# A float32-accurate attention layer on one core: short products placed one by one, and the value products in halves

## The chip, the cores and the metric

The kernel runs on one core of a Trainium2 chip. A core has five engines with queues of their own: TensorE (matrix products into PSUM), VectorE, ScalarE, GpSimd and SyncE, which here issues nearly all DMAs. The metric is the device time of one execution in microseconds. Before the change it was 1571.13 us, the median of three runs (1570.92 to 1571.68).

## The reference

```
w = weights[conditions]                     # 32 of 200 matrices, 128 x 128
x = x + einsum('bct,bcd->bdt', x, w)        # x: 32 x 128 x 1024
# attention over the result: 16 heads of 64, sequence 128
q, k, v = (heads(einsum('bsd,ed->bse', x, W)) for W in (Wq, Wk, Wv))
scores = (q * min(precision, 4)) @ k^T / sqrt(64), causal mask
out = softmax(scores) @ v, heads side by side
x = x + einsum('bsd,ed->bse', out, Wo)      # result: 32 x 128 x 1024, float32
```

## The kernel before

Every float32 operand of a product is split into a high and a low part of the type that TensorE takes at full rate. A product then is three: high by high, high by low, low by high, added up in PSUM (`three`, lines 709 to 712). In most of them 128 rows of weights meet 512 moving columns; these write the banks `PJ` in turn.

TensorE's queue has four stretches. First, for each of the 32 batches, the product by the chosen matrix and its transposition by TensorE (`pe_l0_b`, line 841: a half batch is four transposes of 128 columns into one bank, 256 in all), mixed with the products for V of the first batches. Then the products for V of the other batches, in pairs of batches with seven sums in place of eight (`pe_v_step`), again with transposes in between. Then attention, in 64 cells: a cell is one quarter of the heads' channels of one group of four batches. It has eight steps for Q and eight for K, a step being one `three` of 512 columns, 0.68 us. Beside the steps stand the scores of the cell before (`pe_scores`: four blocks of three products of 256 columns into `SC`) and the value products of an earlier one (`pe_values`, line 815). Last, the output product for one group in full (`pe_out_step`) and for the others in pairs (`pe_product`), which end the kernel.

The value products: P, the normalised exponentials, is turned by VectorE and by DMAs, then split by ScalarE into its high part (L1045) and by GpSimd into its low part (L1336), which stand side by side in `PS`. For each block `u` and each half `h` of the heads one product has V's columns as weights and 256 moving columns, 128 of P's high and 128 of P's low part. PSUM then holds two results side by side, for V's high and low parts in different rows. ScalarE copies "the other rows" (`AC`, L1052 and L1053), VectorE adds the two 128-column results of "the own rows" (L1229, a reduction of 512 elements to 256), GpSimd adds `AC` (L1339), and SyncE stores the sum (L1656). `P` also numbers pairs of blocks: 128 pairs, 512 value products.

What stands where in a queue is set by a table of times: `At.put(t, item)` notes an item at time t in steps, and each engine's program walks over all ticks (`TICK` of them in a step) and issues what is due, in a fixed order of kinds. These times only set the order; on the chip each engine goes on as its semaphores allow. `T_END` is the step at which the steps of Q and K end, `a` the time from which a cell's scores and softmax are counted.

## Time and profile before

| | |
|---|---|
| median of three runs | 1571.13 us |
| span of the profiled execution | 1569.4 us |
| TensorE products, busy | 1559.1 us, 7563 instructions |
| TensorE weight loads, busy | 1311.9 us, 7563 instructions |
| VectorE, ScalarE, GpSimd, busy | 980.4, 818.9, 856.6 us |
| DMA | 341.46 MB, mean 218 GB/s |

The profile is of one execution. PE is TensorE's products, PEld its weight loads, which overlap the products; DVE is VectorE, ACT ScalarE, POOL GpSimd, SPq SyncE's queue of DMA issues. L815 is line 815 of the kernel. A product's duration runs from its start to its modelled end and overlaps the next one's.

### The profile page before, as it was taken

What the parts mean: (1) busy time and instruction counts of PE and PEld (TensorE: products, weight loads), DVE (VectorE), ACT (ScalarE), POOL (GpSimd) and SP (SyncE); (2) the same over time, 40 slices, a digit from 0 to 9 for tenths busy, and PEclk for the clock granted to TensorE, in tenths of its full rate; (3) what the DMA queues carried; (4) which work ended last, traced back from release to release, by engine and by line L of the source; (5) the groups of instructions that cost most, each with busy time, mean ns of one, the idle gap of its engine ahead of it and who ended that gap; (6) DMA issues with size and microseconds to landing.
All of it is one profiled execution on the core that took longest, in us unless ns stands there. A gap on an engine that the chain in (4) does not pass through costs nothing.

```text
span 1569.4 us, 23424 instructions
## 1 busy us (share of the span) xinstructions
PE 1559.1 (99%) x7563; PEld 1311.9 (84%) x7563; DVE 980.4 (62%) x1748; ACT 818.9 (52%) x2221; POOL 856.6 (55%) x752
## 2 busy tenths in 40 slices
PE   9999999999999999999999999999999999999999
PEld 7888888888888888888888888888888878888887
DVE  6844454443367777777766777777777754555553
ACT  6645545543366666666666666666666522222220
POOL 1545645643255566557555566675577544555552
PEclk9999999999999999999999999999999999999999
DMA  9958888865856766667677466666675696444442
GB/s 329 334 212 275 307 285 297 301 214 215 308 182 197 206 207 199 210 188 199 186 240 238 152 172 212 186 182 201 182 195 159 222 367 238 168 161 167 163 163 85
DMA packets 192299, 341.46 MB, mean 218 GB/s; under 512 B 23986, under 2 KB 116402, under 8 KB 185010
## 3 DMA queue, kind: packets, MB, share of 16 engines
q1 hardware_dynamic: 191026, 331.59, 65.8%
q10 hardware_dynamic: 1152, 8.39, 1.4%
q8 instruction: 60, 0.98, 0.3%
q14 instruction: 61, 0.50, 0.1%
HBM read 184.70 MB, written 134.22 MB: 203 GB/s over the span
## 4 chain that ended last, share of the span: by engine, by line
PE 98%; DMA 1%; SPq 1%; POOL 0%; issue 0%; DVE 0%; ACT 0%; DVEq 0%
PE p_PJ L710 22%; PE p_PJ L711 22%; PE p_PJ L712 22%; PE p_SC L712 6%; PE p_SC L711 6%; PE p_SC L710 6%; PE p_PV L815 4%; PE p_LP L710 1%; PE p_PV L710 1%; PE p_PV L712 1%; PE p_PV L711 1%; PE p_LP L711 1%; PE p_LP L712 1%; PE p_PV L841 1%; PE p_LP L841 1%; DMA out<-t_xr 1%
## 5 line engine op out<-in xcount | busy, mean ns | idle before, releaser
L711 PE MATMUL p_PJ<-t_XL,t_WH 128*128 128x512 f32 x1008 | 394.1, 391 | 0.0
L710 PE MATMUL p_PJ<-t_XH,t_WH 128*128 128x512 f32 x1008 | 394.1, 391 | 0.0
L712 PE MATMUL p_PJ<-t_XH,t_WL 128*128 128x512 f32 x1008 | 392.1, 389 | 0.0
L1035 ACT ACTIVATE t_PP<-t_PP,t_st 128x128 f32<-128x128 f32 x512 | 199.5, 391 | 175.4 <-DVE t_st L1211 173.9
L1333 POOL TENSOR_TENSOR t_PP<-t_PP,t_st 128x512 f32<-128x512 f32 x128 | 133.4, 1042 | 205.7 <-DVE t_st L1215 205.7
L712 PEld LDWEIGHTS p_PJ<-t_XH,t_WL 128*128 128x128 f32 x1008 | 189.3, 188 | 40.4
L710 PEld LDWEIGHTS p_PJ<-t_XH,t_WH 128*128 128x128 f32 x1008 | 190.0, 188 | 33.8
L711 PEld LDWEIGHTS p_PJ<-t_XL,t_WH 128*128 128x128 f32 x1008 | 190.0, 188 | 32.3
L1229 DVE TENSOR_REDUCE t_AT<-p_PV 64x256 f32<-64x512 f32 x252 | 171.2, 679 | 23.7 <-ACT t_AC L1053 12.0
L1339 POOL TENSOR_TENSOR t_AT<-t_AT,t_AC 128x256 f32<-128x256 f32 x126 | 117.2, 930 | 125.5 <-DVE t_AT L1229 125.5
L1336 POOL TENSOR_TENSOR t_PS<-t_PT,t_PS 128x512 fp32r<-128x512 f32 x122 | 157.7, 1293 | 0.0
L1205 DVE SCALAR_TENSOR_TENSOR t_PP<-p_SC,t_beta,t_mask 128x256 f32<-128x256 f32 x256 | 111.6, 478 | 44.4 <-PE p_SC L712 44.4
L1322 POOL TENSOR_TENSOR t_xl<-t_XT,t_xh 128x512 fp32r<-128x512 f32 x56 | 74.0, 1322 | 94.9 <-ACT t_xh L917 94.2
L1215 DVE RECIPROCAL t_st<-t_st 128x4 f32<-128x4 f32 x128 | 22.9, 179 | 142.0 <-ACT t_PP L1035 142.0
L1022 ACT ACTIVATE t_KH<-p_PJ 64x512 fp32r<-64x512 f32 x128 | 76.1, 595 | 47.8 <-PE p_PJ L712 46.2
L1052 ACT ACTIVATE t_AC<-p_PV 64x256 f32<-64x256 f32 x128 | 48.9, 382 | 95.9 <-PE p_PV L815 94.4
L1035 ACT ACTIVATION_READ_ACCUMULATOR t_PP<-t_PP,t_st 128x1 f32 x512 | 95.6, 187 | 0.0
L1327 POOL TENSOR_TENSOR t_VV<-t_VX,t_VV 128x512 fp32r<-128x512 f32 x64 | 81.4, 1293 | 25.2 <-ACT t_VV L999 25.2
L1192 DVE TENSOR_TENSOR t_KL<-p_PJ,t_KH 64x512 fp32r<-64x512 f32 x128 | 88.2, 689 | 11.0 <-ACT t_KH L1022 7.0
L1211 DVE TENSOR_REDUCE t_st<-t_PP 128x2 f32<-128x256 f32 x256 | 94.2, 409 | 0.0
L815 PE MATMUL p_PV<-t_PS,t_VV 128*128 128x256 f32 x512 | 82.8, 285 | 3.7 <-POOL t_PS L1336 3.7
L815 PEld LDWEIGHTS p_PV<-t_PS,t_VV 128*128 128x128 f32 x512 | 75.2, 192 | 9.3 <-POOL t_PS L1336 4.1
(254 smaller groups left out, 3545.8 us busy)
## 6 DMA issues: line engine op xcount, KB each, us to landing
t_XH<-xth_scratch SPq DMA_DIRECT2D x56, 512.0 KB, 6.5
t_XL<-xtl_scratch SPq DMA_DIRECT2D x56, 512.0 KB, 6.9
t_PT<-t_TB SPq DMA_DIRECT2D x580, 32.0 KB, 2.3
v_scratch<-t_VR SPq DMA_DIRECT2D x64, 256.0 KB, 4.5
xth_scratch<-t_XH SPq DMA_DIRECT2D x16, 1024.0 KB, 4.0
xtl_scratch<-t_XL SPq DMA_DIRECT2D x16, 1024.0 KB, 6.5
t_VX<-v_scratch SPq DMA_DIRECT2D x32, 512.0 KB, 5.7
at_scratch<-t_AT SPq DMA_DIRECT2D x126, 128.0 KB, 3.5
```

The costliest lines, as they stand in the source:

```text
L710: pe.matmul(bank, lh, rh, start=first, stop=False, skip_group_check=goes_on)
L711: pe.matmul(bank, lh, rl, start=False, stop=False, skip_group_check=goes_on)
L712: return pe.matmul(bank, ll, rh, start=False, stop=last, skip_group_check=goes_on)
L815: mm = pe.matmul(PV2[:, z, 256 * h:256 * h + 256], VV[j % 2][:, u, 2 * c + h, :], moving, start=True, stop=True)
L1035: act.activation(PP[:, u, h, :], PP[:, u, h, :], ACT.Exp, bias=st[:, 0, u, h:h + 1], scale=1.0, accum_out=st[:, 1, u, h:h + 1]).then_inc(a ...
L1192: dve.tensor_tensor(KL[r, :, k], pj[r], KH[r, :, k].bitcast(f32), ALU.subtract).then_inc(dve_k, 1)
L1205: dve.scalar_tensor_tensor(out=PP[:, u], in0=SC[u // 2][:, 256 * (u % 2):256 * (u % 2) + 256].rearrange("p (h k) -> p h k", h=2), scalar=b ...
L1211: dve.tensor_reduce(st[:, 0, u, :], PP[:, u], AX, ALU.max, negate=True).then_inc(dve_m, 1)
L1229: dve.tensor_reduce(at_tile(P)[r], both, AX, ALU.add).then_inc(dve_M, 1)
L1333: pool.tensor_tensor(pp, pp, r, ALU.mult).then_inc(pool_n, 1)
L1336: pool.tensor_tensor(p_half(P, 1), p_raw(P), p_half(P, 0).bitcast(f32), ALU.subtract).then_inc(pool_pt, 1)
L1339: pool.tensor_tensor(at_tile(P), at_tile(P), AC[:, P % 2], ALU.add).then_inc(pool_at, 1)
```

## The change

1. A step is cut into twelve ticks (before four), and each of its three products has a time of its own, a third of a step apart. The output steps get their times from the table too.
2. The transposes, the products of the score blocks and the value products are put into it one by one, a third of a step apart and (by `BETWEEN`) a sixth behind a 512-column product. A cell's scores now take four steps, one block each; the times counted from `a` are one step later. The first eight transposes stay in a row.
3. A value product of 256 columns becomes two of 128, over P's high and then P's low part, with the same weights, added up in the same 128 columns of PSUM. Each pair of blocks has one bank of 512 columns, in turn, where before both banks were shared by all; TensorE waits for the pair before the last, not for the last.
4. VectorE adds the own rows, now 256 columns, and ScalarE's copy of the other rows in one instruction. GpSimd's addition is gone, and with it the semaphore `at_out`; those that waited for it wait for `at_rows`.
5. VectorE's first turn of cell 58 waits for the loads of P as the other cells do, besides the weights' stores.

```diff
 NPAIR = (NG - 1) * GB // 2
 T_OUT = T_PAIR + NPAIR * PAIR
-TICK = 4
+TICK = 12
 T_START = -14
+
+BETWEEN = 1 / 6
...
                     block(kind, n)
                     for d in range(DC):
-                        step_at.put(t0 + 16 * c + 8 * i + d, (kind, n, d))
+                        for m in range(3):
+                            step_at.put(t0 + 16 * c + 8 * i + d + m / 3, (kind, n, d, m))
                 done = t0 + 16 * c + 8
...
                 kl_ev.put(done + 1, n)
-                a = done + 5
+                a = done + 6
                 for u in range(GB):
                     k = u // 2
-                    sc_at.put(a + k, GB * n + u)
+                    for m in range(3):
+                        sc_at.put(a - 1 + u + BETWEEN + m / 3, (GB * n + u, m))
                     mask_at.put(a + 1 + 2 * k, GB * n + u)
                     exp_at.put(a + (2, 3, 4, 5)[u], GB * n + u)
                 move_at.put(a + 10, n)
@@ -390,10 +399,10 @@
                     half_at.put(a + (20 if last else 25.25) + 0.5 * k, P)
                     ptl_at.put(a + (20.75 if last else 26) + 1.5 * k, P)
                     v = a + (27.25 + 3.25 * k if last else 29 + 4.5 * k)
-                    own = v + (1.75 if n >= 4 * NGRP - 2 else (1.75, 8.5)[k])
-                    for z in range(2):
-                        pv_at.put(v, 2 * P + z)
-                    other_at.put(v + 0.75, P)
+                    own = v + (3.25 if n >= 4 * NGRP - 2 else (3.25, 8.5)[k])
+                    for i in range(8):
+                        pv_at.put(v + BETWEEN + i / 3, (2 * P + i // 4, i // 2 % 2, i % 2))
+                    other_at.put(v + 2.25, P)
                     own_at.put(own, P)
                     at_at.put(own + 1.25, P)
 
...
             y_low.put(t + 12.75, b)
 
         turns = [(b, half) for half in (1, 0) for b in range(GB)]
-        x1_load = At()
+        x1_load, out_step, out_add = At(), At(), At()
         for o in range(N_OUT):
+            for d in range(DC):
+                for m in range(3):
+                    out_step.put(T_END + 8 * o + d + m / 3, (o, d, m))
+            out_add.put(T_END + 8 * o + 7.75, o)
...
 
 
+        def value_bank(P):
+
+            return PV[P % 2].rearrange("p (u h q) -> p u h q", u=2, h=2)
...
-        def three(bank, lh, ll, rh, rl, first, last, goes_on=False):
-            pe.matmul(bank, lh, rh, start=first, stop=False, skip_group_check=goes_on)
-            pe.matmul(bank, lh, rl, start=False, stop=False, skip_group_check=goes_on)
+        def one(m, bank, lh, ll, rh, rl, first, last, goes_on=False):
+
+            if m == 0:
+                return pe.matmul(bank, lh, rh, start=first, stop=False, skip_group_check=goes_on)
+            if m == 1:
+                return pe.matmul(bank, lh, rl, start=False, stop=False, skip_group_check=goes_on)
             return pe.matmul(bank, ll, rh, start=False, stop=last, skip_group_check=goes_on)
 
-        def pe_plain_v(n, d):
+        def three(*operands):
+            one(0, *operands)
+            one(1, *operands)
+            return one(2, *operands)
...
-        def pe_values(U):
+            mm = one(m, SC[z][:, 256 * (u % 2):256 * (u % 2) + 256], QH[:, cols], QL[:, cols], KH[:, u, :], KL[:, u, :], True, True)
+            if m == 2:
+                mm.then_inc(pe_sc, 1)
+
+        def pe_values(U, h, a):
             n, u, z = U // GB, U % GB, U % 2
             j, c = divmod(n, NC)
             P = U // 2
-            if z == 0:
+            if z == 0 and h == 0 and a == 0:
                 pe.wait_ge(pool_pt, P + 1)
                 if c == 0:
                     pe.wait_ge(pool_vl, GB * j + u + 2)
-                if P:
-                    pe.wait_ge(dve_M, 2 * P)
-            for h in range(2):
-                moving = PS[:, 2 * u + h].rearrange("p a q -> p (a q)")
-                mm = pe.matmul(PV2[:, z, 256 * h:256 * h + 256], VV[j % 2][:, u, 2 * c + h, :], moving, start=True, stop=True)
-            mm.then_inc(pe_pv, 1)
+                if P >= 2:
+                    pe.wait_ge(dve_M, 2 * (P - 1))
+            mm = pe.matmul(value_bank(P)[:, z, h, :], VV[j % 2][:, u, 2 * c + h, :], PS[:, 2 * u + h, a, :], start=a == 0, stop=a == 1)
+            if h == 1 and a == 1:
+                mm.then_inc(pe_pv, 1)
...
-            for k in range(4):
-                tt = h * 4 + k
-                mm = pe.transpose(bank[:, k * 128:(k + 1) * 128], x_tile(bb)[:, tt * 128:(tt + 1) * 128], ident[:])
-            mm.then_inc(pe_b, 1)
...
+            tt = h * 4 + k
+            mm = pe.transpose(bank[:, k * 128:(k + 1) * 128], x_tile(bb)[:, tt * 128:(tt + 1) * 128], ident[:])
+            if k == 3:
+                mm.then_inc(pe_b, 1)
...
-                for U in pv_at(tick):
-                    pe_values(U)
+                for U, m in sc_at(tick):
+                    pe_scores(U, m)
+                for U, h, a in pv_at(tick):
+                    pe_values(U, h, a)
...
                     if P >= 2:
-                        act.wait_ge(pool_at, P - 1)
-                    act.activation(AC[0:64, k], PV2[64:128, :, 0:128], ACT.Copy).then_inc(act_c, 1)
-                    act.activation(AC[64:128, k], PV2[0:64, :, 256:384], ACT.Copy).then_inc(act_c, 1)
+                        act.wait_ge(dve_M, 2 * (P - 1))
+                    act.activation(AC[0:64, k], value_bank(P)[64:128, :, 0, :], ACT.Copy).then_inc(act_c, 1)
+                    act.activation(AC[64:128, k], value_bank(P)[0:64, :, 1, :], ACT.Copy).then_inc(act_c, 1)
...
-            elif n == 58:
-                dve.wait_ge(s_O, 32 * 32)
             elif k == 0:
                 dve.wait_ge(l_P, 160 * n)
+            if n == 58:
+                dve.wait_ge(s_O, 32 * 32)
...
                         dve.wait_ge(s_at[k], 16 * (P // 2))
                     for h in range(2):
                         r = slice(64 * h, 64 * h + 64)
-                        both = PV2[r, :, 256 * h:256 * h + 256].rearrange("p u (a q) -> p u q a", a=2)
-                        dve.tensor_reduce(at_tile(P)[r], both, AX, ALU.add).then_inc(dve_M, 1)
+                        dve.tensor_tensor(at_tile(P)[r], value_bank(P)[r, :, h, :], AC[r, k], ALU.add).then_inc(dve_M, 1)
...
-                if T_END * TICK <= tick < T_PAIR * TICK and tick % (DC * TICK) == DC * TICK - 1:
-                    o = (tick - T_END * TICK) // (DC * TICK)
+                for o in out_add(tick):
...
-                for P in at_at(tick):
-                    pool.wait_ge(dve_M, 2 * P + 2)
-                    pool.tensor_tensor(at_tile(P), at_tile(P), AC[:, P % 2], ALU.add).then_inc(pool_at, 1)
...
-                    sp.wait_ge(pool_at, P + 1)
+                    sp.wait_ge(dve_M, 2 * P + 2)
```

In attention, around one pair of blocks, TensorE's queue before (L71x are 512-column or score products, L815 value products):

```order
L712 MATMUL p_SC<-t_KH,t_QL 128x256
L710 MATMUL p_SC<-t_KH,t_QH 128x256
L711 MATMUL p_SC<-t_KL,t_QH 128x256
L712 MATMUL p_SC<-t_KH,t_QL 128x256
L815 MATMUL p_PV<-t_PS,t_VV 128x256 [waits at_own_rows,v_low,pt_low]
L815 MATMUL p_PV<-t_PS,t_VV 128x256 x3
L710 MATMUL p_PJ<-t_XH,t_WH 128x512
L711 MATMUL p_PJ<-t_XL,t_WH 128x512
L712 MATMUL p_PJ<-t_XH,t_WL 128x512
```

and now, around a pair of blocks a few cells on (L729 to L732 are the three products of `one`, L840 the value products):

```order
L731 MATMUL p_PJ<-t_XL,t_WH 128x512
L840 MATMUL p_PV<-t_PS,t_VV 128x128
L732 MATMUL p_PJ<-t_XH,t_WL 128x512
L840 MATMUL p_PV<-t_PS,t_VV 128x128
L729 MATMUL p_PJ<-t_XH,t_WH 128x512
L729 MATMUL p_SC<-t_KH,t_QH 128x256 [waits k_low]
L840 MATMUL p_PV<-t_PS,t_VV 128x128
L731 MATMUL p_PJ<-t_XL,t_WH 128x512
L731 MATMUL p_SC<-t_KL,t_QH 128x256
L840 MATMUL p_PV<-t_PS,t_VV 128x128
L732 MATMUL p_PJ<-t_XH,t_WL 128x512
L732 MATMUL p_SC<-t_KH,t_QL 128x256
```

The four value products in a row have become eight, each behind a 512-column product or between one and a score product (`p_SC<-t_KH,t_QH`).

The transposes in the stretch of the V products, before and now (`p_LP` and `p_PV` are banks, `t_XT` the batch):

```order
L711 MATMUL p_PJ<-t_WSL,t_XH 128x512
L712 MATMUL p_PJ<-t_WSH,t_XL 128x512
L841 MATMUL p_LP<-t_ident,t_XT 128x128 [waits l0_x1]
L841 MATMUL p_LP<-t_ident,t_XT 128x128 x3
L710 MATMUL p_PJ<-t_WSH,t_XH 128x512
L711 MATMUL p_PJ<-t_WSL,t_XH 128x512
```

```order
L729 MATMUL p_SC<-t_WSH,t_XH 128x512
L867 MATMUL p_LP<-t_ident,t_XT 128x128 [waits l0_x1]
L731 MATMUL p_SC<-t_WSL,t_XH 128x512
L867 MATMUL p_LP<-t_ident,t_XT 128x128
L732 MATMUL p_SC<-t_WSH,t_XL 128x512
L867 MATMUL p_LP<-t_ident,t_XT 128x128
L729 MATMUL p_SC<-t_WSH,t_SH 128x512 [waits v_out,x_sum_low]
L867 MATMUL p_LP<-t_ident,t_XT 128x128
L731 MATMUL p_SC<-t_WSL,t_SH 128x512
```

Four in a row have become four with one 512-column product between any two.

GpSimd's queue at the end of attention, before and now (`t_PS` is P's low part, for which the value products wait):

```order
L1333 TENSOR_TENSOR t_PP<-t_PP,t_st 128x512 [waits row_recip] x2
L1336 TENSOR_TENSOR t_PS<-t_PT,t_PS 128x4x128 [waits pt_high]
L1339 TENSOR_TENSOR t_AT<-t_AT,t_AC 128x256 [waits at_own_rows]
L1336 TENSOR_TENSOR t_PS<-t_PT,t_PS 128x4x128 [waits pt_high]
L1339 TENSOR_TENSOR t_AT<-t_AT,t_AC 128x256 [waits at_own_rows] x2
L1336 TENSOR_TENSOR t_PS<-t_xr,t_PS 128x4x128 [waits pt_high] x2
L1339 TENSOR_TENSOR t_LATE<-t_LATE,t_AC 128x256 [waits at_own_rows]
L1359 TENSOR_TENSOR t_WR<-t_PP,t_PT 128x512 [waits load_pt,store_wo,load_pair0]
L1339 TENSOR_TENSOR t_LATE<-t_LATE,t_AC 128x256 [waits at_own_rows]
```

```order
L1356 TENSOR_TENSOR t_PP<-t_PP,t_st 128x512 [waits row_recip] x2
L1359 TENSOR_TENSOR t_PS<-t_xr,t_PS 128x4x128 [waits pt_high] x2
L1356 TENSOR_TENSOR t_PP<-t_PP,t_st 128x512 [waits row_recip] x2
L1359 TENSOR_TENSOR t_PS<-t_PT,t_PS 128x4x128 [waits pt_high] x2
L1359 TENSOR_TENSOR t_PS<-t_xr,t_PS 128x4x128 [waits pt_high] x2
L1379 TENSOR_TENSOR t_WR<-t_PP,t_PT 128x512 [waits load_pt,store_wo,load_pair0]
L1382 TENSOR_TENSOR t_WR<-t_WR,t_PP 128x512 [waits pair_sum]
```

The low parts stand directly behind the normalisation (`t_PP<-t_PP,t_st`) or each other; nothing that waits for VectorE's sums (`at_own_rows`) stands between them.

SyncE's queue at the same place, before and now (`t_xr<-t_WR` are the ten moves of the last cell's P, `out<-t_xr` the store of an output row):

```order
L1511 DMA t_LATE<-x_scratch 128x512 [waits store_x1_2,store_x1_1,scores,store_x1_0,y_low]
L1511 DMA t_xr<-x_scratch 128x512 [waits store_out0]
L1530 DMA t_xr<-t_WR 32x256 [waits pt_low,p_turned]
L1530 DMA t_xr<-t_WR 32x256 x9
L1680 DMA out<-t_xr 128x512 [waits out_row]
L1656 DMA at_scratch<-t_AT 128x256 [waits at_out]
L1511 DMA t_xr<-x_scratch 128x512 [waits store_out1]
L1656 DMA at_scratch<-t_AT 128x256 [waits at_out]
```

```order
L1531 DMA t_LATE<-x_scratch 128x512 [waits store_x1_2,store_x1_1,scores,store_x1_0,y_low]
L1531 DMA t_xr<-x_scratch 128x512 [waits store_out0]
L1699 DMA out<-t_xr 128x512 [waits out_row]
L1550 DMA t_xr<-t_WR 32x256 [waits pt_low,p_turned]
L1550 DMA t_xr<-t_WR 32x256 x9
L1676 DMA at_scratch<-t_AT 128x256 [waits at_rows]
L1531 DMA t_xr<-x_scratch 128x512 [waits store_out1]
L1676 DMA at_scratch<-t_AT 128x256 [waits at_rows]
```

The store of one output row has moved from behind the ten moves to ahead of them.

## Rows read from the trace of the kernel before

**Rows 1.** The page: engines, and the chain that ended last.
```profile
PE 1559.1 (99%) x7563; PEld 1311.9 (84%) x7563; DVE 980.4 (62%) x1748; ACT 818.9 (52%) x2221; POOL 856.6 (55%) x752
...
PE 98%; DMA 1%; SPq 1%; POOL 0%; issue 0%; DVE 0%; ACT 0%; DVEq 0%
```
**Rows 2.** The page's costliest groups: busy us, mean ns of one, idle before.
```profile
L1339 POOL TENSOR_TENSOR t_AT<-t_AT,t_AC 128x256 f32<-128x256 f32 x126 | 117.2, 930 | 125.5 <-DVE t_AT L1229 125.5
...
L815 PE MATMUL p_PV<-t_PS,t_VV 128*128 128x256 f32 x512 | 82.8, 285 | 3.7 <-POOL t_PS L1336 3.7
```
**Rows 3.** Timeline of TensorE in attention: start us, duration us.
```profile
450.21 0.28 PE L710 MATMUL p_SC<-t_KH,t_QH 128*128 128x256 f32 x1
...
450.93 0.40 PE L710 MATMUL p_PJ<-t_XH,t_WH 128*128 128x512 f32 x1
...
452.33 0.64 PE L815 MATMUL p_PV<-t_PS,t_VV 128*128 128x256 f32 x4
452.81 0.40 PE L710 MATMUL p_PJ<-t_XH,t_WH 128*128 128x512 f32 x1
...
453.28 0.39 PE L712 MATMUL p_PJ<-t_XH,t_WL 128*128 128x512 f32 x1
...
459.87 0.39 PE L711 MATMUL p_PJ<-t_XL,t_WH 128*128 128x512 f32 x1
```
**Rows 4.** The same timeline, the weight load at 450.93.
```profile
450.93 0.19 PEld L711 LDWEIGHTS p_PJ<-t_XL,t_WH 128*128 128x128 f32 x1
```
**Rows 5.** Timeline of loads, then of products, after TensorE had been idle.
```profile
80.18 0.19 PEld L710 LDWEIGHTS p_PJ<-t_WSH,t_SH 128*128 128x128 f32 x1 [1.05 <-issue]
80.29 0.19 PEld L711 LDWEIGHTS p_PJ<-t_WSL,t_SH 128*128 128x128 f32 x1
...
80.22 0.47 PE L710 MATMUL p_PJ<-t_WSH,t_SH 128*128 128x512 f32 x1 [0.66 <-issue]
80.52 0.39 PE L711 MATMUL p_PJ<-t_WSL,t_SH 128*128 128x512 f32 x1
```
**Rows 6.** Timeline of TensorE around four transposes.
```profile
85.55 0.39 PE L712 MATMUL p_PJ<-t_WSH,t_SL 128*128 128x512 f32 x1
85.78 0.60 PE L841 MATMUL p_LP<-t_ident,t_XT 128*128 128x128 f32 x4
86.13 0.47 PE L710 MATMUL p_PJ<-t_WSH,t_SH 128*128 128x512 f32 x1
86.45 0.39 PE L711 MATMUL p_PJ<-t_WSL,t_SH 128*128 128x512 f32 x1
...
86.11 0.19 PEld L710 LDWEIGHTS p_PJ<-t_WSH,t_SH 128*128 128x128 f32 x1
86.22 0.19 PEld L711 LDWEIGHTS p_PJ<-t_WSL,t_SH 128*128 128x128 f32 x1
```
**Rows 7.** The transposes by line: duration ns, least, median, most.
```profile
L841 PE MATMUL p_LP<-t_ident,t_XT x120: 270/272/273, 10.9 to 370.3; 128*128 128x128 f32 x120
```
**Rows 8.** Timeline of all engines at the end of attention.
```profile
1262.37 6.28 SPq L1530 DMA_DIRECT2D t_xr<-t_WR  x10
...
1271.04 0.63 ACT L1045 ACTIVATE t_PS<-t_xr 128x512 fp32r<-128x512 f32 x1 [5.75 <-DMA t_xr<-t_WR]
...
1271.48 1.41 DVE L1229 TENSOR_REDUCE t_AT<-p_PV 64x256 f32<-64x512 f32 x2 [5.58 <-DMA at_scratch<-t_AT]
...
1272.96 0.72 POOL L1339 TENSOR_TENSOR t_AT<-t_AT,t_AC 128x256 f32<-128x256 f32 x1 [8.65 <-DVE t_AT L1229]
1273.65 2.49 POOL L1336 TENSOR_TENSOR t_PS<-t_xr,t_PS 128x512 fp32r<-128x512 f32 x2
1274.96 1.23 PE L815 MATMUL p_PV<-t_PS,t_VV 128*128 128x256 f32 x4 [3.67 <-POOL t_PS L1336]
```
**Rows 9.** Stretches there: busy us (count) by engine, then granted clock.
```profile
1275.00:1281.00 6.00, 6.00 (x19) 5.08 (x20) 1.38 (x2) 0.85 (x3) 1.87 (x2) 0.52 0.99 363
1281.00:1290.00 9.00, 9.00 (x41) 7.46 (x40) 6.37 (x7) 3.51 (x7) 5.57 (x4) 1.00 1.09 387
```

More of the change, by code:

```diff
@@ L274, in plan_l0 @@
                 l0_x1.put(q + 3.75, (bb, h))
-                l0_b.put(q + 5, (bb, h))
+                for k in range(4):
+                    l0_b.put(q + 5 + BETWEEN + k / 3, (bb, h, k))
                 l0_X.put(q + 5.75, (bb, h))
@@ L291, in plan_l0_pair @@
                 l0_x1.put(q + 0.75, (bb, h))
-                l0_b.put(q + 5, (bb, h))
+                for k in range(4):
+                    l0_b.put(q + 5 + BETWEEN + k / 3, (bb, h, k))
                 l0_X.put(q + (6.5, 5.75)[h], (bb, h))
@@ L304, in cond_attention @@
             l0_x1.put(-4 + h, (0, h))
-            l0_b.put(-3 + h, (0, h))
+            for k in range(4):
+                l0_b.put(-3 + h, (0, h, k))
             l0_X.put(-2 + 0.75 * h, (0, h))
@@ L732, in pe_step @@
             n = 0 if kind == "q" else 1
-            if d == 0:
+            if d == 0 and m == 0:
                 pe_wait_bank(kind, item)
@@ L754, in pe_step @@
             z = x_at_(j)
-            mm = three(PJ[bank_of[kind, item]][:], lh, ll, x_chunk(XHP, z, d), x_chunk(XLP, z, d), d == 0, d == DC - 1)
-            if d == DC - 1 and kind == "q":
+            mm = one(m, PJ[bank_of[kind, item]][:], lh, ll, x_chunk(XHP, z, d), x_chunk(XLP, z, d), d == 0, d == DC - 1)
+            if d == DC - 1 and m == 2 and kind == "q":
                 mm.then_inc(pe_q, 1)
-            elif d == DC - 1:
+            elif d == DC - 1 and m == 2:
                 mm.then_inc(pe_k, 1)
@@ L854, in pe_out_step @@
             quarter = ((0, 2), (1, 3))[half][row // 4]
-            if b == 0 and d % 4 == 0:
+            if b == 0 and d % 4 == 0 and m == 0:
                 pe.wait_ge(l_O[quarter], 32)
@@ L858, in pe_out_step @@
             rh, rl = wo_tile(quarter)
-            mm = three(PJ[bank_of["o", o]][:], XH[1][:, row, cols], XL[1][:, row, cols], rh[:, d % 4, :], rl[:, d % 4, :], d == 0, d == DC - 1)
-            if d == DC - 1:
+            mm = one(m, PJ[bank_of["o", o]][:], XH[1][:, row, cols], XL[1][:, row, cols], rh[:, d % 4, :], rl[:, d % 4, :], d == 0, d == DC - 1)
+            if d == DC - 1 and m == 2:
                 mm.then_inc(pe_o, 1)
@@ L891, in pe_program @@
             for tick in range(T_START * TICK, (T_OUT + 4) * TICK):
-                for kind, item, d in step_at(tick):
-                    pe_step(kind, item, d)
-                for p, i, d in P_at(tick):
-                    pe_v_step(p, i, d)
-                pe_out_step(tick)
+                for kind, item, d, m in step_at(tick):
+                    pe_step(kind, item, d, m)
+                for p, i, d, m in P_at(tick):
+                    pe_v_step(p, i, d, m)
+                for o, d, m in out_step(tick):
+                    pe_out_step(o, d, m)
                 for q, i in R_at(tick):
@@ L1675, in sp_program @@
                     sp_load_x1(o)
-                if T_END * TICK <= tick < T_PAIR * TICK and tick % (DC * TICK) == DC * TICK - 1:
-                    o = (tick - T_END * TICK) // (DC * TICK)
+                for o in out_add(tick):
                     b, half = turns[o]
```

62 lines of the change are left out of this document (30 added, 32 removed).

## The prediction

> **What bounds the kernel now.** I read the page's head first: TensorE's products are busy 99% of the span, VectorE 62%, GpSimd 55%, and the chain of waits that ended last is 98% TensorE, most of it the products into the three projection banks [rows 1]. So time is saved or lost only where TensorE's own queue gets shorter or longer, or stands still. Busy time is no help for the price of a product, since products overlap in it (a 256-column one is "busy" 285 ns [rows 2]); the price is the step from one start to the next. The order of starts gives it: 29 products of 512 columns from 453.28 to 459.87 us, 227 ns each; six of 256 columns (two score blocks) from 450.21 to 450.93, 120 ns each; the four value products from 452.33 to 452.81, again 120 ns [rows 3]. The difference of 107 ns for 256 columns is 53.5 ns per 128, so a product costs its columns at the full clock and 13.3 ns besides. By that line a product of 128 columns would cost 66.5 ns.
>
> But every product has its own weight load. In the timeline the load of the next product starts in the same moment as the product before it (450.93 and 450.93) and never sooner, however long that product is [rows 3, 4]: one set of weights is in use, one can be loaded. How long a load takes is seen where the engine had been idle: the load starts at 80.18, its product is given as started at 80.22 but lasts 0.47 us, and the load for the product after it starts at 80.29; the product after it at 80.52, a normal 0.23 us later [rows 5]. So 0.11 us pass from the start of a load until its product really runs. Under 227 or 120 ns this is hidden; under 53.5 ns it isn't. The one kind of 128-column product that is there, the transposes, says the same: after a 512-column product at 85.55, four of them start at 85.78, the next 512-column product is put at 86.13 with 0.47 us instead of 0.39, and the following one starts at 86.45 [rows 6]. From 85.55 to 86.45 are 0.90 us for two long and four short products: (0.90 - 2 x 0.227) / 4 = 111 ns per transpose, not 66.5. Within the group it is 109: four in 0.60 us, the last one's own 272 ns taken off, over three [rows 7]. And behind the last of them, load 86.11 to load 86.22, an ordinary product's weights took 0.11 us too.
>
> **The change, part by part.**
>
> *Value products.* 512 products of 256 columns go [rows 2] and 1024 of 128 columns come, each with its own load (TensorE has 512 instructions more). They stand one by one behind a 512-column product, or next to a score product. That placing hides the short product's own load, under the long one. It does not hide the load of the product that follows, which can start only when the short one starts, and so the short one's slot lasts as long as that load. Bounds: 66.5 ns from below (the line through [rows 3]), 120 ns from above, what a 256-column slot costs, load included. The nearest rows are the load of 0.11 us [rows 5] and the step behind a transpose, 86.22 less 86.11, with the long product's start a few ns off; I take 113 ns. Before: 512 x 0.120 = 61.4 us. After: 1024 x 0.113 = 115.7 us. That is +54.3 us, all on the path, since nothing else runs on this engine meanwhile. At 109 ns it is +50.2, at 120 ns +61.5.
>
> *Score products.* 768 of 256 columns, three per block, now one by one. Their slot of 120 ns is longer than the load of 110, so there was nothing exposed; I count 0. The recorded starts shift by some 6 ns at a change from long to short and back, so ±4.6 us (768 x 6 ns) is the bound.
>
> *Transposes.* 256 in all (32 batches, two halves, four each); 248 now stand in between. Before 256 x 0.111 = 28.4 us; at 113 ns after, +0.5 us; at 120 ns +2.3. The last of a group now stands 1.17 steps of 0.68 us behind the first, not directly behind it: the splits that wait for them come 0.8 us later at most. In the opening three batches are near their due time; 0 to 1 us, I take 0.
>
> *VectorE, ScalarE, GpSimd.* The sums of P's halves over 512 PSUM columns become additions over 256, and 126 additions of GpSimd, 930 ns each, go [rows 2]. Neither engine holds TensorE up in the steady part: in front of all 512 value products it waited 3.7 us in total [rows 2], and this was a single wait (below). The 117 us of GpSimd's work are worth nothing by themselves. The added condition on PSUM is looser: the value products now wait for the pair before last, not the last.
>
> *The single wait.* At the end of attention TensorE stands still for 3.67 us before the value products at 1274.96, and the granted clock falls: 0.52 on average from 1275 to 1281, against 1.00 in the stretch behind it [rows 8, 9]; (1 - 0.52) x 6 = 2.9 us more. Followed back: P's low half on GpSimd (L1336, 1273.65) stands in its queue behind the addition L1339 (1272.96), which waits for VectorE's L1229 (1271.48), which waited for a store. ScalarE had the high half ready at 1271.04 + 0.63 = 1271.67. With the addition gone, the low half can start there, 2.0 us sooner. Against it: the ten moves of P (L1530, 0.6 us each from 1262.37) now stand behind one more output store, +0.6 us. TensorE itself comes about 1.1 us later to that place (one step, and eight short products more). So 3.67 - 2.0 + 0.6 - 1.1 = 1.2 us of waiting stay, and with so short a stop I expect the clock to hold: idle time before the product at 80.22 was 0.66 us and the steps behind it are normal [rows 5]. Gain 2.5 + 2.9 = 5.4, I take 5; at most 3.67 + 2.9 = 6.6, at least 0.
>
> Sum: 54.3 + 0.5 + 0 - 5 = +49.8 us on a span of 1569.4, 1619.2; the median of the runs, 1571.1, lies 1.7 above that span, so **1621 us**.
>
> Two rules of the Trainium skill speak against this. "TensorE: Matmul & The Clock Gate", in "Back-to-back issue gap", gives for a sustained stream of load and product pairs some 81 ns at 128 columns and 131 ns at 512. The trace doesn't agree on the second: 227 ns [rows 3]. By the first, 1024 value products would cost 82.9 us, an estimate, and the change some +9 in place of +50. The same page's "Step-by-step: what each phase is for" has loads pulled ahead of products in flight by a window of 64 instructions. Here they are ahead by one product and no more [rows 4]; were they further ahead, the case "hidden" below would hold.
>
> **Rivals.** With s for the slot of a 128-column product in us, all of it is 1280 s - 61.4 - 28.4 - 5 = 1280 s - 94.8 on top of 1571.1. The point between gain and loss is s = 0.074.
> - *Hidden.* Loads run further ahead once long products stand between; a short product costs its columns and the 13.3 ns, s = 0.0665, for the transposes too: 85.1 - 94.8 = -9.7, 1561 us. That is the faster side, and it decides below 74 ns. If the fixed 13.3 ns went as well, for the scores too, -26 - 10: 1535. For it: a group of short ones is where loads pile up now. Against: load behind product by product, and 0.11 us from an idle engine, where nothing was in its way.
> - *Partly hidden.* s midway between 0.0665 and 0.109, 0.088: 112.6 - 94.8 = +17.8, 1589 us, with 1580 at s = 0.080. For it only that no row has an ordinary product of 128 columns: a transpose could be slow of itself, and a load from an idle engine slower than one beside a product. Against: the 0.11 us of the load behind the transposes [rows 6].
> - *Load and fixed part add.* s = 0.109 + 0.013 = 0.122: +61.4, 1632 us. For it: the 13.3 ns sit on every slot seen, and 120 ns for 256 columns could be read as just this. Against: 111 ns for the transposes.
> - *The stop at the end stays* or moves elsewhere: +5, 1626, inside the first case's own range.
>
> **Numbers.** Load-bound (1621): 0.65, own range 1609 to 1640. Load plus fixed part (1632): 0.16. Partly hidden (1589): 0.05. Hidden (1561 and below): 0.14. A range of 1580 to 1640 leaves out the hidden case and a little above. What a measurement can tell from no change is about 0.2%, 3 us. Faster by more than that 0.12, within it 0.02, slower 0.86.
>
> **What would show it.** In the profile after: load starts of the product behind a value product, equal to the value product's start, and 0.11 us on the next load; start to start of a pair long plus short near 0.34 us (0.29 would be the hidden case, 0.31 the partly hidden case); scores still 0.347 per pair of long and short; a pair of value and score product 0.23. The total of TensorE's queue from the first to the last value product longer by some 54 us; between 1280 us and the end nothing changed. GpSimd's low halves at the end directly behind ScalarE's, and no slice of lower clock there. I am wrong if the long-plus-short step is under 0.31, or if TensorE waits in every cell for halves or for the PSUM additions.

## The result and the profile after

The changed kernel takes 1647.38 us, median of four runs (1646.79 to 1649.29); before, on the same chip, 1571.03 (1570.33 to 1571.68). The ratio is 1.0489, 95% interval 1.0474 to 1.0504: +76.4 us, where +50 was forecast. The sign was right, the time lies outside the range.

The profiled span went from 1569.4 to 1646.1 us. The page of the changed kernel, engines (busy us, share, count), the chain that ended last and its second line, and groups as in [rows 2]:

```profile
PE 1629.7 (99%) x8075; PEld 1359.4 (83%) x8075; DVE 941.3 (57%) x1748; ACT 813.5 (49%) x2221; POOL 758.1 (46%) x624
...
PE 70%; DVE 11%; ACT 7%; issue 6%; POOL 3%; DMA 2%; SPq 1%; ACTq 0%; DVEq 0%
...
L840 PE MATMUL p_PV<-t_PS,t_VV 128*128 128x128 f32 x1024 | 228.0, 223 | 1.8 <-POOL t_PS L1359 1.8
```

The busy share of TensorE is 99% as in [rows 1] and tells nothing. The chain does: 98% TensorE became 70%, and VectorE, ScalarE and GpSimd stand in it with 21%. Something in the steady part now waits. It isn't in the product rows, whose only wait in attention is the single one at its end, but in those of the weight loads. The waits of TensorE's loads in the changed kernel (waiter, what it waited for: us in total, times, longest):

```profile
PEld p_SC L729 <- DVE t_KL L1217: 22.1, 49, 0.6
```

49 times the first score product of a cell waits for K's low part from VectorE. Before there was no such row. The timeline of one of the places, TensorE with a load among its products (start us, duration us, ..., idle before and what ended it):

```profile
701.75 0.22 PE L840 MATMUL p_PV<-t_PS,t_VV 128*128 128x128 f32 x1
701.81 0.44 PE L732 MATMUL p_PJ<-t_XH,t_WL 128*128 128x512 f32 x1
702.09 0.22 PE L840 MATMUL p_PV<-t_PS,t_VV 128*128 128x128 f32 x1
702.15 0.44 PE L729 MATMUL p_PJ<-t_XH,t_WH 128*128 128x512 f32 x1
...
702.73 0.19 PEld L729 LDWEIGHTS p_SC<-t_KH,t_QH 128*128 128x128 f32 x1 [0.45 <-DVE t_KL L1217]
...
702.73 0.38 PE L729 MATMUL p_SC<-t_KH,t_QH 128*128 128x256 f32 x1
702.95 0.22 PE L840 MATMUL p_PV<-t_PS,t_VV 128*128 128x128 f32 x1
```

Two things are to be read here. First the short product: from 702.09 to 702.15 and from there 0.28 us as a rule (701.81 to 702.09), so a pair of long and short takes 0.34 us as forecast, against 0.227 for the long one alone. The recorded starts split it as 0.06 and 0.28, because the long product is "started" when it is issued and runs when its weights are in. Second the wait: the product at 702.15 is followed after 0.58 us, not 0.28. Since the product before overlaps the gap, TensorE shows no idle time. And the score product after the wait has a slot of 0.22 us (702.73 to 702.95), not 0.12: its load began only now and isn't hidden.

VectorE at the same place in the changed kernel, and GpSimd's row for which its second turn waits:

```profile
697.61 1.04 POOL L1356 TENSOR_TENSOR t_PP<-t_PP,t_st 128x512 f32<-128x512 f32 x1 [1.81 <-DVE t_st L1240]
...
698.68 0.71 DVE L1127 STREAM_TRANSPOSE t_TB<-t_PP 128x512 f32<-128x512 f32 x1 [0.54 <-POOL t_PP L1356]
...
699.32 1.12 DVE L1259 TENSOR_TENSOR t_OL<-t_xr,t_OH 128x512 fp32r<-128x512 f32 x1
...
700.37 0.86 DVE L1253 TENSOR_TENSOR t_AT<-p_PV,t_AC 64x256 f32<-64x256 f32 x2
...
701.26 1.41 DVE L1217 TENSOR_TENSOR t_KL<-p_PJ,t_KH 64x512 fp32r<-64x512 f32 x2
```

and the same cell before, with its first score product:

```profile
670.92 1.29 DVE L1102 STREAM_TRANSPOSE t_TB<-t_PP 128x512 f32<-128x512 f32 x2
672.13 1.37 DVE L1229 TENSOR_REDUCE t_AT<-p_PV 64x256 f32<-64x512 f32 x2
673.53 0.69 DVE L1235 TENSOR_TENSOR t_OL<-t_xr,t_OH 128x512 fp32r<-128x512 f32 x1
674.26 1.41 DVE L1192 TENSOR_TENSOR t_KL<-p_PJ,t_KH 64x512 fp32r<-64x512 f32 x2
...
676.77 0.28 PE L710 MATMUL p_SC<-t_KH,t_QH 128*128 128x256 f32 x1
```

Counted from the start of K's last product (671.96 before, 697.89 after): VectorE's turns of P end at +0.25 before and +1.50 after; K's low part begins at +2.30 and +3.37 and ends at +3.71 and +4.78. The first score product stood at +4.81 before, a slack of 1.10 us (the time between a result and the product that takes it). After, without its wait of 0.30, it would stand at +4.54: late by 0.30 with the 0.06 from VectorE's end to the load. The second turn comes 1.25 us later, since it waits for GpSimd's normalisation (L1356), and that for a softmax counted one step later whose scores now come one block per step. Behind it in VectorE's queue stand, before and after, the split of Wo's or another weight (L1259), the own rows and K's low part. The own rows got 0.5 us shorter (1.37 to 0.86), the split 0.43 us longer (0.69 to 1.12).

Where the span went: to the first score product 411.7 before and 413.7 after (+2.0); the 63 stretches from a cell's first score product to the next one's 838.1 and 912.8 (+74.7); the rest 319.6 and 319.6. A stretch was 13.33 us in all cells from the third on; now it is 14.63 us in 41 of 59 cells, 14.20 in 9 and between the two in the others. The rest is equal by accident: 42 of the 1024 halves lie in it (before 20 of the 512 whole products), some 2.4 us more, and the stop at the end of attention is shorter (below).

### The profile page after: what moved, and what is told of

Its sections match the earlier page's. It is cut to its first block, busy times and chain, and to the rows that moved or that the text cites. A ratio compares the mean times of both kernels' runs of the same rounds, so it can differ in the third digit from the quotient of the medians.

```text
span 1646.1 us, 24320 instructions
## 1 busy us (share of the span) xinstructions
PE 1629.7 (99%) x8075; PEld 1359.4 (83%) x8075; DVE 941.3 (57%) x1748; ACT 813.5 (49%) x2221; POOL 758.1 (46%) x624
## 4 chain that ended last, share of the span: by engine, by line
PE 70%; DVE 11%; ACT 7%; issue 6%; POOL 3%; DMA 2%; SPq 1%; ACTq 0%; DVEq 0%
PE p_PJ L732 14%; PE p_PJ L731 14%; PE p_PJ L729 13%; PE p_SC L729 7%; PE p_SC L732 6%; PE p_SC L731 6%; DVE t_KL L1217 4%; ACT t_PP L1060 4%; POOL t_PP L1356 3%; PE p_PV L840 3%; DVE t_AT L1253 2%; DVE t_OL L1259 1%; ACT t_QH L1055 1%; PE p_LP L729 1%; PE p_PV L729 1%
## 5 line engine op out<-in xcount | busy, mean ns | idle before, releaser
L731 PE MATMUL p_PJ<-t_XL,t_WH 128*128 128x512 f32 x1008 | 410.7, 407 | 0.0
L732 PE MATMUL p_PJ<-t_XH,t_WL 128*128 128x512 f32 x1008 | 408.1, 405 | 0.0
L729 PE MATMUL p_PJ<-t_XH,t_WH 128*128 128x512 f32 x1008 | 404.0, 401 | 0.0
L1356 POOL TENSOR_TENSOR t_PP<-t_PP,t_st 128x512 f32<-128x512 f32 x128 | 133.1, 1040 | 498.3 <-DVE t_st L1240 498.3
L840 PE MATMUL p_PV<-t_PS,t_VV 128*128 128x128 f32 x1024 | 228.0, 223 | 1.8 <-POOL t_PS L1359 1.8
L729 PEld LDWEIGHTS p_PJ<-t_XH,t_WH 128*128 128x128 f32 x1008 | 189.7, 188 | 37.5
L732 PEld LDWEIGHTS p_PJ<-t_XH,t_WL 128*128 128x128 f32 x1008 | 189.8, 188 | 33.9
L840 PEld LDWEIGHTS p_PV<-t_PS,t_VV 128*128 128x128 f32 x1024 | 194.9, 190 | 8.1 <-POOL t_PS L1359 2.2
L1253 DVE TENSOR_TENSOR t_AT<-p_PV,t_AC 64x256 f32<-64x256 f32 x252 | 105.4, 418 | 137.3 <-ACT t_AC L1078 126.7
L1359 POOL TENSOR_TENSOR t_PS<-t_PT,t_PS 128x512 fp32r<-128x512 f32 x122 | 176.3, 1466 | 0.0
L1220 DVE TENSOR_TENSOR t_QL<-p_PJ,t_QH 128x512 fp32r<-128x512 f32 x64 | 44.2, 691 | 123.9 <-ACT t_QH L1055 123.9
L1127 DVE STREAM_TRANSPOSE t_TB<-t_PP 128x512 f32<-128x512 f32 x116 | 81.8, 705 | 32.7 <-POOL t_PP L1356 32.4
L1217 DVE TENSOR_TENSOR t_KL<-p_PJ,t_KH 64x512 fp32r<-64x512 f32 x128 | 88.1, 688 | 8.7 <-ACT t_KH L1047 4.7
L729 PE MATMUL p_SC<-t_KH,t_QH 128*128 128x256 f32 x256 | 79.9, 312 | 6.9
```

The costliest lines, as they stand in the source:

```text
L729: return pe.matmul(bank, lh, rh, start=first, stop=False, skip_group_check=goes_on)
L731: return pe.matmul(bank, lh, rl, start=False, stop=False, skip_group_check=goes_on)
L732: return pe.matmul(bank, ll, rh, start=False, stop=last, skip_group_check=goes_on)
L840: mm = pe.matmul(value_bank(P)[:, z, h, :], VV[j % 2][:, u, 2 * c + h, :], PS[:, 2 * u + h, a, :], start=a == 0, stop=a == 1)
L1127: dve.transpose(turned(n)[:, :, 4 * k:4 * k + 4, :], pp).then_inc(dve_t, 1)
L1217: dve.tensor_tensor(KL[r, :, k], pj[r], KH[r, :, k].bitcast(f32), ALU.subtract).then_inc(dve_k, 1)
```

## The experiments

In what follows, "a cell" is that stretch, from the recorded starts of the trace. Each time has its ratio to the kernel before on the same chip.

**Only the halves.** The kernel before, each value product as two of 128 columns in a row into the old places in PSUM, nothing else:

```diff
-                moving = PS[:, 2 * u + h].rearrange("p a q -> p (a q)")
-                mm = pe.matmul(PV2[:, z, 256 * h:256 * h + 256], VV[j % 2][:, u, 2 * c + h, :], moving, start=True, stop=True)
+                for a0, a1 in ((0, 128), (128, 256)):
+                    moving = PS[:, 2 * u + h].rearrange("p a q -> p (a q)")[:, a0:a1]
+                    mm = pe.matmul(PV2[:, z, 256 * h + a0:256 * h + a1], VV[j % 2][:, u, 2 * c + h, :], moving, start=True, stop=True)
```

> The kernel before with one edit: each value product of 256 columns is issued as two of 128 columns with the same weights, in a row, results side by side as before. Theory L (a short product's slot is the next product's weight load, 0.115 us, wherever it stands): 1024 x 0.115 - 512 x 0.120 = +56 us, 1627 us; the step in a row of eight is 0.11 to 0.12 us in the timeline. Rival A (columns plus a fixed 13 ns, and the 76 us are all placing and waits): 1024 x 0.0665 - 61.4 = +7, 1578 us. Rival P (short products cost more one by one than in a row): between, under 1610 us.

1626.63 us (1626.25 to 1627.7), ratio 1.0354 (1.0337 to 1.0371); cell 14.21 us. 16 halves take what 8 products of 0.120 took and 0.88 more: (0.957 + 0.88) / 16 = 0.1148 us each. Eight of them in a row, with the products around them:

```profile
690.50 0.39 PE L712 MATMUL p_PJ<-t_XH,t_WL 128*128 128x512 f32 x1
690.73 1.00 PE L816 MATMUL p_PV<-t_PS,t_VV 128*128 128x128 f32 x8
691.57 0.45 PE L710 MATMUL p_PJ<-t_XH,t_WH 128*128 128x512 f32 x1
691.86 0.40 PE L711 MATMUL p_PJ<-t_XL,t_WH 128*128 128x512 f32 x1
```

**Unequal halves.** As before, but of 64 and 192 columns: `((0, 64), (64, 256))`.

> The kernel before with each value product of 256 columns as one of 64 and one of 192 columns. Theory L: both slots are a weight load of 0.115 us, since 192 columns take 0.080 + 0.013 = 0.093 us, so the same +56 us as with two of 128, 1627 us. Rival A (columns plus fixed part): +7 us, 1578. Rival C (a short product has a cost that grows as it gets shorter, or with the columns): different from the 128 + 128 kernel by more than 5 us.

1627.48 us, ratio 1.0361 (1.0344 to 1.0378); the cell 14.21 us, the same to the nanosecond. Within a row the steps are 51 and 172 ns, 223 in all for the two, as with two equal halves, and the loads start 0.11 us apart in both kernels: the number of loads decides, not how the columns are shared out.

**Fewer weight columns.** Only the halves, but the second of each with 64 columns of weights in place of 128 (rows 64 to 127 of P's low part's result are left out):

```diff
+                for a0, rows in ((0, 128), (128, 64)):
+                    moving = PS[:, 2 * u + h].rearrange("p a q -> p (a q)")[:, a0:a0 + 128]
+                    mm = pe.matmul(PV2[0:rows, z, 256 * h + a0:256 * h + a0 + 128], VV[j % 2][:, u, 2 * c + h, 0:rows], moving, start=True, stop=True)
```

> As the kernel with two value products of 128 columns in a row, but the second of each two uses only 64 of the 128 columns of weights, so rows 64 to 127 of P's low part's result are not computed. Theory L1 (the load takes 0.11 us for 128 columns of weights, in proportion to them): the slot before it falls from 0.113 to its own 0.067, 512 x 0.046 = 24 us less than 1627, 1603 us. Theory L2 (a load takes 0.11 us whatever its width): 1627.

1599.47 us, ratio 1.0177 (1.0162 to 1.0193); cell 13.76 us. From the start of a 64-column load to the start of the next load 62 ns pass on average, from that of a 128-column load 111. Of the 55.5 us that the halves add 27 are gone, with every second load half as wide:

```profile
682.52 0.39 PE L712 MATMUL p_PJ<-t_XH,t_WL 128*128 128x512 f32 x1
682.74 0.80 PE L816 MATMUL p_PV<-t_PS,t_VV 128*128 128x128 f32 x8
683.38 0.44 PE L710 MATMUL p_PJ<-t_XH,t_WH 128*128 128x512 f32 x1
```

From the first short product to the long one 0.64 us, above 0.84. The price of a short product is the next one's load. The result is 3.5 us under the 1603 that I expected: the slot that a 64-column load leaves, 2 x 0.087 - 0.115 = 0.059 us by the cell, is less than the 0.067 that the prediction's line (columns and 13.3 ns) gives to a product of 128 columns. The narrow products also write 64 rows of PSUM in place of 128; this run alone doesn't separate that from their loads.

**The own rows behind K's low part.** The changed kernel, one number:

```diff
-                    own = v + (3.25 if n >= 4 * NGRP - 2 else (3.25, 8.5)[k])
+                    own = v + (3.25 if n >= 4 * NGRP - 2 else (3.25, 10)[k])
```

> The changed kernel with VectorE's addition of the own rows for the second pair of blocks of a cell moved 1.5 steps back, behind the low part of K. Theory W (49 of 64 cells make TensorE wait 0.41 us for the low part of K, which stands in VectorE's queue behind this addition): the wait goes, cells shrink from 14.6 to 14.2 us, 1647 - 20 = 1627 us. Rival (the wait comes from the score blocks being spread, which makes the softmax and VectorE's turn of P late; the addition is innocent): the wait stays in half or more, above 1637 us.

1627.16 us, ratio 1.0359 (1.0342 to 1.0376); cell 14.20 us in all 59 cells from the third to the 61st. 20 us of the 76 are gone by one place in VectorE's queue. VectorE in the same cell, K's low part now ahead of the own rows:

```profile
691.25 0.71 DVE L1127 STREAM_TRANSPOSE t_TB<-t_PP 128x512 f32<-128x512 f32 x1 [0.54 <-POOL t_PP L1356]
691.88 1.12 DVE L1259 TENSOR_TENSOR t_OL<-t_xr,t_OH 128x512 fp32r<-128x512 f32 x1
692.93 1.40 DVE L1217 TENSOR_TENSOR t_KL<-p_PJ,t_KH 64x512 fp32r<-64x512 f32 x2
694.36 0.88 DVE L1253 TENSOR_TENSOR t_AT<-p_PV,t_AC 64x256 f32<-64x256 f32 x2
...
694.99 0.28 PE L729 MATMUL p_SC<-t_KH,t_QH 128*128 128x256 f32 x1
```

694.33 to 694.99 are 0.66 us of slack.

**The scores in a row again.** The changed kernel with `a = done + 5` and `sc_at.put(a + k, ...)` for all three products of a block.

> The changed kernel with the score products in rows of six at the places of before and the softmax's times one step earlier, as before; value products and transposes stay one by one. Theory W (one step of delay in VectorE's queue makes K's low part late): the softmax, the turns and the additions are one step earlier, the wait goes: about 1627 us. Theory L adds that score products cost 0.120 us in a row or not, so no further change. If placing scores one by one saved time: above 1630 us even without the wait.

1626.64 us, ratio 1.0351 (1.0334 to 1.0368); cell 14.20 us, equal to that of the experiment before. With the softmax counted from where it was, the turn is early enough, and the wait is gone though the own rows still stand ahead of K's low part; the slack is 0.67 us. So there are two ways out of it. This one takes back the later softmax and the spread scores together; what each is worth alone it doesn't tell. In the cells the placing of the scores costs nothing beside the halves; the 0.3 us less in attention lie in the first two cells.

**The values in a row.** As "the own rows behind", and the eight halves of a pair of blocks in a row: `pv_at.put(v, ...)`.

> The changed kernel with the late addition (the kernel that ran at 1627 us) and the eight value products of 128 columns of a pair of blocks in a row, not one by one between products of 512 columns. Theory L: every short slot is a load of 0.11 us wherever it stands: within 3 us of 1627. If placing short products between long ones hid anything: slower than 1635. If it costs something (the load and start of a long product behind a short one): 1622 or less.

1631.4 us (1629.26 to 1631.86), ratio 1.0382 (1.0366 to 1.0397); cell 14.25 us. That is 4.2 us above the kernel with the own rows behind, where I had expected at most 3. Placing the halves one by one is worth 0.05 us in a cell, 3 us in all, against rows of eight with the scores spread. This fits score products that cost 6 ns more when alone, and something less when a value product stands beside them; it isn't shown by itself.

**Placing alone, three times.** The changed kernel's placing with whole value products of 256 columns, and the sums as before (VectorE's reduction, GpSimd's addition); in the first `own = v + (2, 7)[k]`:

```diff
                     for i in range(8):
-                        pv_at.put(v + BETWEEN + i / 3, (2 * P + i // 4, i // 2 % 2, i % 2))
+                        if i % 2 == 0:
+                            pv_at.put(v + BETWEEN + i / 6, (2 * P + i // 4, i // 2 % 2, 0))
```

> Placing alone: short products one by one as in the changed kernel, but the value products whole, 256 columns, with the sums of VectorE and GpSimd as before (own rows early enough not to stand ahead of K's low part). Theory L: a 256-column slot of 0.120 us covers its load, so placing brings nothing: 1571 us, plus 1 to 3 for the later start of attention and the spread scores, 1572 to 1575. Rival H (placing hides loads, for scores and transposes too): 1560 or less. Rival W2 (spreading the scores itself makes TensorE wait): 1580 or more.

1662.48 us, ratio 1.0576 (1.0562 to 1.0591). I had expected no wait. The waits of its products:

```profile
PE p_PV L842 <- POOL t_PS L1362: 72.6, 63, 2.1
```

My earlier own rows put GpSimd's addition ahead of P's low half, in a queue where it waits for VectorE. So I took back the times of before (`a = done + 5`, own rows at 8.5), the spread scores beginning at `a - 1`:

> The placing alone, without the halves: transposes, score products and value products one by one behind 512-column products as in the changed kernel, but value products of 256 columns and the sums as before (VectorE's reduction, GpSimd's addition of the other rows), and the times counted from `a` as before, so that VectorE has K's low part done in the same place as before. Theory P (placing hides nothing, since a slot is as long as the load of the next product, and a score product that stands alone costs 6 ns more): 1571.2 + 766 x 0.006 = 1575.8 us, value pair with a long one still 0.347 us, no new wait. Rival H (placing hides part of a short product): under 1569 us. Rival W2 (the placing itself makes waits, as in the kernel with whole products of the last run: 1662): over 1590 us, with a wait for GpSimd's low parts or for K's low part in most of the 64 cells.

1597.77 us, ratio 1.0170 (1.0155 to 1.0186). Missed again: now the scores begin 0.83 of a step earlier than before, and K's low part is late in 48 cells by a wait of its own:

```profile
PEld p_SC L730 <- DVE t_KL L1219: 19.4, 48, 0.4
PEld p_PV L842 <- issue: 22.5, 63, 1.2
```

The second line is another wait. In all 59 cells from the third on the first value product comes 0.32 us or more behind its long product, in place of 0.227, and always 0.15 us behind the end of VectorE's own rows of the pair before: it waits for them, as it does more plainly in the next kernel. So the 26.8 us are two waits, each with a load laid bare, and the scores' 6 ns, and not K's low part alone, as the next expectation takes it.

Last, the same with the scores from `a - 1/3` on:

> As the last kernel with whole value products placed one by one (1597.8 us, where K's low part was late in most cells because the spread scores began 0.83 of a step earlier than before), but the spread scores begin at the place where they began before (a sixth of a step sooner). Theory P (placing hides nothing; a score product that stands alone costs 6 ns more; all the rest of the 26.8 us was the wait for K's low part): 1571.2 + 766 x 0.006 = 1575.8 us, 1574 to 1578, slack between K's low part and the first score product positive in nearly all cells. Rival W2 (the placing itself costs more, wait or no wait): over 1582 us. Rival H (placing hides part of a short product): under 1570 us.

1602.74 us, ratio 1.0195 (1.0178 to 1.0212). K's low part has 0.37 us of slack or more in every cell, and yet a cell takes 13.82 us, 0.49 more than before. In 61 cells the first value product follows its long product after 0.57 us in place of 0.227. In the products' waits it shows as

```profile
PE p_PV L842 <- DVE t_AT L1256: 11.3, 61, 0.2
```

With whole products all pairs share both banks, and the own rows of the pair before aren't read in time; 0.35 us. The rest is the late product's own load, which nothing hides (its slot is 0.19 us in place of 0.12), and 12 x 0.006 for the scores (pair with a long one 0.353 us, before 0.347): 0.35 + 0.07 + 0.07 = 0.49. Theory P had it right that placing hides nothing, and wrong that it costs only the scores. I never got placing alone without a wait. What the three show together is that a spread row shifts what stands around it. In the changed kernel the first value product of 48 cells starts 0.85 us before the own rows of the pair before are done. On shared banks it would have had to wait for them; the two banks in turn spare it that, not the placing.

**The stop at the end.** The kernel before with one addition of GpSimd behind P's low parts, and one load of x three steps earlier, so that its store passes the moves:

```diff
-                    at_at.put(own + 1.25, P)
+                    at_at.put(own + (3 if P == 8 * NGRP - 3 else 1.25), P)
...
-            x1_load.put(T_END + ((-4, -4, 8, 10)[o] if o < 4 else 8 * o - 20), o)
+            x1_load.put(T_END + ((-4, -4, 8, 10, 17)[o] if o < 5 else 8 * o - 20), o)
```

> The kernel before with two items of the end of attention moved: GpSimd's addition for the last pair but two behind P's low parts, and the load of output row 4's x behind the moves of the last P in SyncE's queue, so that these don't wait for a store to land. Nothing is added or taken away. Theory E (3.67 us of standing still and the 2.9 us that the halved clock costs behind it are both due to this wait): 1571 - 6.6 = 1565 us. If only the wait goes and the clock falls all the same: 1568. If the wait moves on to the next pair: 1571.

1571.32 us against 1571.30, ratio 0.9998 (0.9989 to 1.0007). The addition alone:

> The kernel before with one addition of GpSimd (the other rows of pair 125, L1339) placed behind P's low parts of the last cell, nothing else. Theory E (the stop at the end is worth its 3.7 us and the lost clock, if nothing else is moved): the stop shrinks by about 1.5 us and the time falls by 1.5 us, or by 4.4 us if the clock holds: 1566.8 to 1569.8 us. Rival S (what follows waits for the last cell's other transfers anyway): 1571.2 +- 0.7 us, the stretch after attention longer by as much as the stop is shorter.

1570.79 against 1570.94, ratio 1.0000 (0.9991 to 1.0009). Both shortened the stop of 3.67 us [rows 8]; the product behind it, of the first kernel, then of the second:

```profile
1273.97 0.74 PE L815 MATMUL p_PV<-t_PS,t_VV 128*128 128x256 f32 x4 [2.17 <-POOL t_PS L1336]
```

```profile
1274.48 0.74 PE L815 MATMUL p_PV<-t_PS,t_VV 128*128 128x256 f32 x4 [2.73 <-POOL t_PS L1336]
```

In the first the clock even held: the stretch of [rows 9] reads

```profile
1275.00:1281.00 6.00, 5.66 (x27) 4.46 (x26) 2.75 (x4) 1.26 (x4) 1.59 (x3) 1.00 0.95 354
```

and the last value product starts at 1277.55 us, not 1280.46. But each has a new wait in the output stretch, for VectorE's output row (the products' waits of either):

```profile
PE p_SC L710 <- DVE t_xr L1261: 2.0, 1, 2.0
```

```profile
PE p_SC L710 <- DVE t_xr L1261: 1.3, 1, 1.3
```

From the last value product to the end the first kernel takes 292.9 us, the one before 289.0, 3.9 more. Of these 2.0 are the new wait, and behind it the clock fell after all:

```profile
1316.00:1322.00 6.00, 6.00 (x21) 4.82 (x20) 2.15 (x4) 1.67 (x3) 2.55 (x2) 0.72 0.36 131
```

That is (1 - 0.72) x 6 = 1.7 us. The stop and its clock moved on by some 40 us into the output; the expectation's third case, 1571 us, had the time right and the place (the next pair) wrong. That the same output work simply is reached earlier, while its transfers aren't earlier, fits; which transfer it is I didn't settle. In the second kernel the stretch behind is 1.4 us longer and the last value product 1.4 us earlier, as rival S says. No version found here beats the kernel before.

## Why the prediction was partly wrong

- **The halves: right.** Slot forecast 113 ns, measured 114.8 in the cells; +54.3 us forecast, +55.5 by the experiment that does only this. The bounds (109 to 120) held. That the price is the load behind, and not the columns, was shown twice, by unequal halves and by narrower weights (with the reserve on rows of PSUM). The rivals "hidden", "partly hidden" and "load and fixed part add" fall. The line "its columns at the full clock and 13.3 ns besides" was drawn through 512 and 256 columns and doesn't reach to 128: there a product took 59 ns where its successor's load allowed it, not 66.5. Nothing in the sum hung on that.
- **The failed step** is the sentence "Neither engine holds TensorE up in the steady part", from which VectorE, ScalarE and GpSimd were put at 0. Its evidence was the wait in front of the value products; it says nothing of how soon the score products need K's low part. The sentence was true of the kernel before. What it left out is how long they would go on not doing so: K's low part had 1.10 us of slack (the cell of both kernels shown above), and the change counts softmax, turns and second own rows one step of 0.68 us later and spreads the scores over four, with K's low part left at its time. With the longer split ahead of it, that moved it 1.07 us back, while the score product came 0.27 us sooner. Cost: 0.30 us of waiting and 0.11 us of exposed load in each of 49 cells, 20 us; one number in the table takes it back (1647.4 to 1627.2 us). The prediction named this as what would make it wrong ("if TensorE waits in every cell"), for halves or PSUM additions, but gave it no price and no chance.
- **Score products:** 0 forecast, at most 4.6. Alone they are 6 ns slower where that could be isolated (whole value products); beside the halves the cells show no cost.
- **Transposes:** +0.5, and the opening between 0 and 1 and taken as 0; the first score product came 2.0 us later. Kernels that changed nothing there have it at 411.5 to 412.4 us, those with the transposes spread at 413.3 to 414.4. So the forecast was 1 to 1.5 us too low.
- **The stop at the end:** forecast 1.2 us of waiting left and the clock held. Measured:

```profile
1352.19 0.33 PE L840 MATMUL p_PV<-t_PS,t_VV 128*128 128x128 f32 x1 [1.79 <-POOL t_PS L1359]
...
1352.00:1358.00 6.00, 5.81 (x24) 5.01 (x25) 0.88 (x3) 0.76 (x2) 1.38 (x2) 0.72 0.92 350
```

  1.79 us of waiting and (1 - 0.72) x 6 = 1.7 us of clock, 3.5 together against 6.6: a gain of 3.1, not 5. The clock fell though the idle time was half of what it had been. The low half came directly behind ScalarE's high half, as forecast, and this alone is the 1.9 us by which the wait shrank. The two terms beside it, +0.6 for the moves and -1.1 for a later TensorE, cancelled: the high half began 0.24 us before TensorE ran dry (1350.16 and 1350.40), 0.25 in the kernel before.
- **The sum, done again:** 55.5 (halves) + 20 (new wait) + 2 (opening) - 3 (stop) = 74.5, of 76.4. The other 1.9 us I can't assign.
- **GpSimd's 117 us: right.** With its addition gone (own rows behind K's low part) and with it still there (only the halves), the cells take 14.20 and 14.21 us.

## What to carry over

Price a short product by the load of the product behind it: columns of weights, not of data. Before an engine off the path is put at 0, read its slack where the path takes its result, and set against it every later start that the change gives to what stands ahead in its queue; an engine with 57% busy time was late in 49 of 64 cells. Look for waits in the weight-load rows too, since products that overlap the gap hide them, and let experiments on placing keep each neighbour's order, or they measure another wait.

## What the runs showed of the hardware

- A load of 128 weight columns takes 0.11 us. One of 64 takes at most 0.06: its product's 128 columns may have set that bound. The load follows TensorE's clock: at the lower of the two levels, 1.2 GHz (granted clock 0.50 from 1353.5 to 1356.5), behind the stop in the changed kernel, long and short together take 0.64 us:

```profile
1354.59 0.31 PE L840 MATMUL p_PV<-t_PS,t_VV 128*128 128x128 f32 x1
1354.69 0.73 PE L731 MATMUL p_PJ<-t_WL,t_XH 128*128 128x512 f32 x1
1355.23 0.31 PE L840 MATMUL p_PV<-t_PS,t_VV 128*128 128x128 f32 x1
```

  A long one alone takes 0.43 us at that level, in the kernel before (granted clock 0.50 from 1276 to 1277):

```profile
1276.41 0.63 PE L711 MATMUL p_PJ<-t_WL,t_XH 128*128 128x512 f32 x1
1276.84 0.63 PE L712 MATMUL p_PJ<-t_WH,t_XL 128*128 128x512 f32 x1
```

  So 0.64 - 0.43 = 0.21 us are left for the short one, about twice the load of before.
- The clock held behind stops of 2.17 and 2.45 us (the end of attention moved; own rows behind K's low part) and fell behind one of 1.79 us (the changed kernel). The length of the stop alone doesn't decide. The second of them:

```profile
1331.00:1337.00 6.00, 5.01 (x29) 4.39 (x30) 1.64 (x4) 1.26 (x3) 2.16 (x2) 1.00 0.96 332
```
- VectorE's split of a weight (`t_OL`, both inputs in SBUF) takes 0.69 us in the kernel before and 1.13 in all 48 places after, where it runs beside GpSimd's split of P (L1359). Those 48 of GpSimd's splits take 1.73 us, all its others 1.29. K's low part (L1217, one input in PSUM) runs beside the same kind of split in 76 places and still takes 0.68. Before, the weight's split ran beside GpSimd's addition: VectorE kept its 0.69 us, and the addition took 1.24 us there, 0.73 to 0.76 everywhere else. So not every pair of VectorE and GpSimd instructions slows down, and not always both sides. The inputs in SBUF are the difference seen between the weight's split and K's low part; that they are the cause no run shows.
